# Attention block kernel: the stream of row maxima moved by 69 of a group's 144 events

## What is computed

```python
logits = jnp.einsum('bhqd,bhkd->bhqk', q, k) / jnp.sqrt(jnp.float32(HEAD))
causal = jnp.tril(jnp.ones((seq_len, seq_len), dtype=bool))
logits = jnp.where(causal[None, None], logits, -jnp.inf)
attn = jax.nn.softmax(logits, axis=-1)
o = jnp.einsum('bhqk,bhkd->bhqd', attn, v)
```

## Time and profile before

| what | value |
|---|---|
| median of 3 runs | 1465.85 us (1465.51 to 1467.76) |
| span of the profiled execution | 1465.0 us |
| mean granted TensorE clock of it | 0.921 |
| TensorE busy (matmuls) | 1309.6 us, 89% |
| VectorE busy | 1022.1 us, 70% |
| ScalarE busy | 773.8 us, 53% |
| prologue of the maxima | about 142 to 232 us |
| groups 0 to 7 | about 232 to 1112 us |

### The profile page before, as it was taken

How to read it: one execution, slowest core, us unless ns; L and a number is a source line. 1 busy time by engine, 2 the same in 40 slices (tenths; PEclk the granted TensorE clock), 3 DMA queues, 4 the chain that set the end, 5 groups by cost and what they waited for, 6 DMA issues and landing times. The chain is left out here.

```text
span 1465.0 us, 25799 instructions
## 1 busy us (share of the span) xinstructions
PE 1309.6 (89%) x8432; PEld 679.2 (46%) x8432; DVE 1022.1 (70%) x1862; ACT 773.8 (53%) x1009; POOL 172.6 (12%) x101
## 2 busy tenths in 40 slices
PE   4993899999999998999998999999994599999997
PEld 3872223333333333333433433433221588888886
DVE  4893997886886885886887688688300466666664
ACT  2771004665665664666565666566793244444443
POOL 1468100000000000000000000000001122222221
PEclk8996557999999999999999999999997699999999
DMA  6345400002102101200210300200003102222200
GB/s 204 123 165 165 131 1 11 21 16 58 33 18 50 40 17 35 56 19 15 65 26 4 74 18 16 63 6 5 10 8 91 44 1 58 58 57 57 57 14 29
DMA packets 75812, 71.07 MB, mean 49 GB/s; under 512 B 17816, under 2 KB 68704, under 8 KB 75688
## 3 DMA queue, kind: packets, MB, share of 16 engines
q1 hardware_dynamic: 75688, 69.51, 16.9%
HBM read 47.57 MB, written 21.23 MB: 47 GB/s over the span
## 5 line engine op out<-in xcount | busy, mean ns | idle before, releaser
L854 DVE TENSOR_REDUCE mx<-ps 128x1 f32<-128x512 f32 (+3 forms) x1120 | 692.2, 669 | 170.8 <-PE ps L726 105.8
L808 ACT ACTIVATE prob<-ps 128x1024 f32<-128x1024 f32 (+3 forms) x640 | 546.7, 895 | 413.8 <-PE ps L751 260.0
L723 PE MATMUL ps<-kst,qst 96*128 96x512 bf16 (+3 forms) x1280 | 426.4, 374 | 28.4 <-DMA kst<-qk_parts 24.3
L747 PE MATMUL ps<-qst,kst 99*128 99x512 bf16 (+3 forms) x1280 | 362.2, 355 | 11.2 <-issue 7.5
L763 PE MATMUL ps<-prob,vw 128*32 128x512 f32 (+3 forms) x2560 | 303.8, 547 | 0.2
L723 PEld LDWEIGHTS ps<-kst,qst 96*128 96x128 bf16 x1280 | 120.7, 99 | 334.7 <-DVE mx L854 244.9
L747 PEld LDWEIGHTS ps<-qst,kst 99*128 99x128 bf16 x1280 | 118.9, 99 | 147.5 <-ACT prob L808 51.1
L751 PE MATMUL ps<-mask_k,ident_bf 128*128 128x128 bf16 x512 | 106.2, 227 | 0.0
L726 PE MATMUL ps<-mask_q,ident_bf 128*128 128x128 bf16 x512 | 106.0, 232 | 0.0
L926 POOL COPY vw<-v_nat 128x1024 f32 (+1 forms) x8 | 8.3, 1044 | 766.3 <-PE ps L763 766.3
L763 PEld LDWEIGHTS ps<-prob,vw 128*32 128x32 f32 x2560 | 51.0, 109 | 102.0 <-issue 79.6
(11 more groups left out here) (144 smaller groups left out, 1429.5 us busy)
## 6 DMA issues: line engine op xcount, KB each, us to landing
qk_parts<-parts SPq DMA_DIRECT2D x32, 384.0 KB, 2.9
qst<-qk_parts SPq DMA_DIRECT2D x192, 64.0 KB, 2.6
kst<-qk_parts SPq DMA_DIRECT2D x192, 64.0 KB, 2.5
xs<-in_x SPq DMA_DIRECT2D x16, 512.0 KB, 6.3
o_rows<-o_sb SPq DMA_DIRECT2D x128, 32.0 KB, 1.7
o_raw<-o_rows SPq DMA_DIRECT2D x16, 256.0 KB
rd<-rden_rows SPq DMA_DIRECT2D x16, 256.0 KB
out<-y SPq DMA_DIRECT2D x8, 512.0 KB, 3.2
```

The source lines that it names most:

```text
L723: last = pe.matmul(at, q[0:QK_ROWS, J, h0 + h, i % 4 * P:(i % 4 + 1) * P], k[0:QK_ROWS, cb, h0 + h, 0:width], start=True, stop=not diagonal)
L747: last = pe.matmul(ps[:, h, 0:width], kst[c][0:ST_ROWS, t // 4, h, t % 4 * P:(t % 4 + 1) * P], qst[c][0:ST_ROWS, J, h, skip:BLK], start=Tr ...
L808: act.activation(prob[:, n % P_BUFS, 2 * pair:2 * pair + 2, 0:width], ps[:, 2 * pair:2 * pair + 2, 0:width], ACT.Exp).then_inc(exp_done, 1)
L854: dve.tensor_reduce(mx[:, h0:h0 + nh, i % 4, cb], ps[:, bank, 0:nh * width].rearrange("p (h x) -> p h x", h=nh), AX, ALU.max).then_inc(max ...
```

## The change

The stream of events is cut at event 69. The prologue holds events 0 to 68 of group 0. In group s the 120 slots hold events 69 to 143 of group s itself, then events 0 to 68 of group s + 1, spread evenly over all slots (1.2 per slot); group 7 holds only its own 75. So the turns of J = 2 and 3 (events 86 and 143) come in slots 14 and 62 of their own group, those of J = 0 and 1 (events 14 and 42) in slots 74 and 98 of the group ahead. `sync_step` has a new order to match, `invert` is called earlier in the stream of events, and the loads of group 1's queries and keys stand behind the maxima rows of J = 0 and 1 of group 0.

```diff
@@ -90,19 +74,21 @@
 EV = max_events()
 NEV = len(EV)
 assert NEV % S_BUFS == 0
-FIRST_SLOT = 7
 SLOTS_OF_TILE = 3
 
 
+
+AHEAD = 69
+TURN_EVENT = [EV.index(("turn", J)) for J in range(NJ)]
+NEAR_UNITS = [J for J in range(NJ) if TURN_EVENT[J] < AHEAD]
+OWN_UNITS = [J for J in range(NJ) if TURN_EVENT[J] >= AHEAD]
+INVERT_AT = NMU // 4
+
+
 def event_slots():
 
-    slots, done = [], 0
-    for u in range(SLOTS_OF_TILE * NKT):
-        want = min(NEV, max(0, (u - FIRST_SLOT) * NEV // (SLOTS_OF_TILE * NKT - FIRST_SLOT - 2)))
-        slots.append(range(done, want))
-        done = want
-    slots[-1] = range(slots[-1].start, NEV)
-    return slots
+    count = SLOTS_OF_TILE * NKT
+    return [range(u * NEV // count, (u + 1) * NEV // count) for u in range(count)]
 
 
 SLOTS = event_slots()
@@ -665,44 +651,59 @@
 
 
 
-            def sync_step(sp, s, c, hs, cur, nxt, far):
-                nhs = hs + c
-                nc_ = 1 - c
-                for J in range(NJ):
-                    if nxt:
-                        sp.wait_ge(max_red, (s + 1) * NEV + EV.index(("turn", J)) + 1)
-                        for a in range(NPART):
-                            sp.dma_start(qst[nc_][QK_ROWS + a:QK_ROWS + a + 1, J],
-                                         mT[a * 16:(a + 1) * 16, J, :]).then_inc(m_in[nc_][J], 16)
-                    if cur and far and J < NJ - 1:
-
+            def load_maxima(sp, s, c, J):
+
+                sp.wait_ge(max_red, s * NEV + TURN_EVENT[J] + 1)
+                for a in range(NPART):
+                    sp.dma_start(qst[c][QK_ROWS + a:QK_ROWS + a + 1, J],
+                                 mT[a * 16:(a + 1) * 16, J, :]).then_inc(m_in[c][J], 16)
+
+            def store_out(sp, s, c, hs, J):
+
+                sp.wait_ge(o_out, s * NJ + J + 1)
+                cols = slice(c * S + J * BLK, c * S + (J + 1) * BLK)
+                for h in range(GH):
+                    sp.dma_start(o_rows[bass.ds(hs * GH + h, 1), :, cols]
+                                 .rearrange("o r t -> (o r) t"),
+                                 o_sb[2 * HD * h:2 * HD * h + HD, J % 2, :]
+                                 ).then_inc(o_stored[J % 2], 16)
+
+                    sp.dma_start(den[32 * J + 8 * h:32 * J + 8 * h + 8, c, :],
+                                 o_sb[2 * HD * h + HD:2 * HD * h + HD + 1, J % 2, :]
+                                 ).then_inc(den_in[J % 2], 16)
+
+            def sync_step(sp, s, c, hs, nxt, far):
+
+                def queries(J):
+                    if far:
                         sp.wait_ge(st_done, s * 2 * NKT + 2 * (1 + max(n for n in range(NKT) if KT[n][0] == J)))
                         load_q(sp, c, hs + 1, J)
-                    if cur and far and J == NJ - 1:
-
-                        sp.wait_ge(st_done, (s + 1) * 2 * NKT)
-                        for j in range(NJ):
-                            load_k(sp, c, hs + 1, j)
-                        load_q(sp, c, hs + 1, J)
-                    if cur:
-                        sp.wait_ge(o_out, s * NJ + J + 1)
-                        cols = slice(c * S + J * BLK, c * S + (J + 1) * BLK)
-                        for h in range(GH):
-                            sp.dma_start(o_rows[bass.ds(hs * GH + h, 1), :, cols]
-                                         .rearrange("o r t -> (o r) t"),
-                                         o_sb[2 * HD * h:2 * HD * h + HD, J % 2, :]
-                                         ).then_inc(o_stored[J % 2], 16)
-
-                            sp.dma_start(den[32 * J + 8 * h:32 * J + 8 * h + 8, c, :],
-                                         o_sb[2 * HD * h + HD:2 * HD * h + HD + 1, J % 2, :]
-                                         ).then_inc(den_in[J % 2], 16)
-                    if cur and J == 1 and not (isinstance(s, int) and s == 0):
-                        store_rden(sp, s - 1, 1 - c, hs - 1 + c)
+
+                load_maxima(sp, s, c, OWN_UNITS[0])
+                for J in NEAR_UNITS:
+                    queries(J)
+                    store_out(sp, s, c, hs, J)
+                for J in OWN_UNITS[1:]:
+                    load_maxima(sp, s, c, J)
+                for J in OWN_UNITS[:-1]:
+                    queries(J)
+                    if nxt:
+                        load_maxima(sp, s + 1, 1 - c, NEAR_UNITS[0])
+                    store_out(sp, s, c, hs, J)
+                for J in NEAR_UNITS[1:]:
+                    if nxt:
+                        load_maxima(sp, s + 1, 1 - c, J)
+                if not (isinstance(s, int) and s == 0):
+                    store_rden(sp, s - 1, 1 - c, hs - 1 + c)
+                if far:
+                    sp.wait_ge(st_done, (s + 1) * 2 * NKT)
+                    for j in range(NJ):
+                        load_k(sp, c, hs + 1, j)
+                    load_q(sp, c, hs + 1, NJ - 1)
+                store_out(sp, s, c, hs, NJ - 1)
 
             def tensor_step(pe, s, c, hs, cur, nxt):
-                g, q, k = s + 1, qst[1 - c], kst[1 - c]
-
-                def event(e):
+                def event(g, gc, gh, e):
                     kind, w = EV[e]
                     bank = S_BANK + e % S_BUFS
 
@@ -716,12 +717,12 @@
                         return
                     J, i, h0, nh, cb, width, diagonal = MU[w]
                     if w == 0 or MU[w - 1][0] != J:
-                        pe.wait_ge(q_in[1 - c][J], loads(hs + c, Q_DMAS))
-                        pe.wait_ge(k_in[1 - c][J], loads(hs + c, K_DMAS))
+                        pe.wait_ge(q_in[gc][J], loads(gh, Q_DMAS))
+                        pe.wait_ge(k_in[gc][J], loads(gh, K_DMAS))
                     for h in range(nh):
                         at = ps[:, bank, h * width:(h + 1) * width]
-                        last = pe.matmul(at, q[0:QK_ROWS, J, h0 + h, i % 4 * P:(i % 4 + 1) * P],
-                                         k[0:QK_ROWS, cb, h0 + h, 0:width], start=True, stop=not diagonal)
+                        last = pe.matmul(at, qst[gc][0:QK_ROWS, J, h0 + h, i % 4 * P:(i % 4 + 1) * P],
+                                         kst[gc][0:QK_ROWS, cb, h0 + h, 0:width], start=True, stop=not diagonal)
                         if diagonal:
                             last = pe.matmul(at[:, width - P:width], ident_bf[:], mask_q[:],
                                              start=False, stop=True)
@@ -729,7 +730,10 @@
 
                 def maxima(slot):
                     for e in SLOTS[slot]:
-                        event(e)
+                        if AHEAD + e < NEV:
+                            event(s, c, hs, AHEAD + e)
+                        elif nxt:
+                            event(s + 1, 1 - c, hs + c, AHEAD + e - NEV)
 
                 def logits(n, pair):
                     J, t = KT[n]
@@ -766,22 +770,19 @@
                     last.then_inc(pv_done, 1)
 
                 if not cur:
-                    for e in range(NEV):
-                        event(e)
+                    for e in range(AHEAD):
+                        event(s + 1, 1 - c, hs + c, e)
                     return
                 for n in range(NKT):
                     logits(n, 0)
-                    if nxt:
-                        maxima(SLOTS_OF_TILE * n)
+                    maxima(SLOTS_OF_TILE * n)
                     if n >= PV_LAG:
                         values(n - PV_LAG, s, c)
                     elif not (isinstance(s, int) and s == 0):
                         values(NKT + n - PV_LAG, s - 1, 1 - c)
-                    if nxt:
-                        maxima(SLOTS_OF_TILE * n + 1)
+                    maxima(SLOTS_OF_TILE * n + 1)
                     logits(n, 1)
-                    if nxt:
-                        maxima(SLOTS_OF_TILE * n + 2)
+                    maxima(SLOTS_OF_TILE * n + 2)
                 if not nxt:
                     for n in range(NKT - PV_LAG, NKT):
                         values(n, s, c)
@@ -857,7 +858,7 @@
                         if w in LAST_MU:
                             dve.wait_ge(max_red, g * NEV + e + 1)
                             make_parts(LAST_MU[w])
-                        if w == NMU // 2 and not (isinstance(s, int) and s <= 0):
+                        if w == INVERT_AT and not (isinstance(s, int) and s <= 0):
                             invert(dve, s - 1, 1 - c)
                     assert count[0] == per_s
 
@@ -878,17 +879,18 @@
                 for J in range(NJ):
                     load_q(sp, 0, 0, J)
                     load_k(sp, 0, 0, J)
+                for J in NEAR_UNITS:
+                    load_maxima(sp, 0, 0, J)
                 for J in range(NJ):
                     load_q(sp, 1, 0, J)
                     load_k(sp, 1, 0, J)
-                sync_step(sp, -1, 1, -1, False, True, False)
-                sync_step(sp, 0, 0, 0, True, True, True)
+                sync_step(sp, 0, 0, 0, True, True)
                 with sp.Fori(0, (NG - 4) // 2) as k:
```

(10 more changed lines are left out.)

## The result

The changed kernel takes 1416.2 us (median of 3 runs, 1415.77 to 1416.47) against 1465.85: a ratio of 0.9653, 95% interval 0.9636 to 0.9671. That is 49.6 us less, where 29.4 were forecast. The profiled execution spans 1414.0 us.

The account below looks back on a forecast made before the run. TensorE was taken as the bound in middle groups, VectorE in the late prologue. Terms -45.9 + 16.2 - 6.5 - 3.2 + 2 + 3 + 5 = -29.4 gave 1436.4 us against the median; range 1423 to 1454.

Parts of the forecast that it names:

- step 8: Full tiles: spreading events evenly, 3.6 a tile instead of 4, costed at nothing.
- step 4: Turn of J 3, seven groups: logits before it cut the pause from 1.96 to about 1.5 us, -3.2 us.
- step 7: Middle of groups: pauses among full tiles lower the clock in three of ten cases, +5 us (bounds 0 and 17).
- Step 1: Prologue: only 69 events remain, so group 0 starts near 186.2 instead of 232.1, -45.9 us.
- Step 2: Group 7: 75 events in tiles 0 to 20 make it 96.0 us against 79.8, +16.2 us.
- Step 3: Starts of groups: low clock in groups 1, 2, 6 and group 4's wait for keys go, -6.5 us.
- step 6: Middle of groups 3 and 5: VectorE's loop ends make TensorE idle 1.5 us each, +3 us.
- Step 5: Start of group 0: low clock as before (7.9 us), now with events in these tiles, +2 us.
- Step 9: SyncE's queue: maxima loads arrive in time for tile 12, with 2 to 5 us of cover.
- Rival B: Turns of J 0 to 2: spread dissolves their waits (8.4 us), no clock falls (-5): 1423 us, chance 0.12.
- Rival A: Full tiles: all ten pauses bring the low clock, VectorE's loop ends cost in full: 1452 us, chance 0.16.
- Rival C: Group 0: clock doesn't rise, all of it runs at 1.2 GHz: 1531 us, chance 0.04.

Follow-up runs that it names:

- run 3: Changed kernel with its shift by 69 events but the old uneven slots (first eight empty, then 1.3 events a slot): 1434.35 us.
- run 4: Changed kernel with the old uneven slots, and the turn of J 3 one slot later, behind a pair of logits: 1433.74 us.
- run 1: Changed kernel with the turn of J 3 moved into the slot of its last unit, no logits between: 1424.99 us.
- run 6: Changed kernel with VectorE's three passes written out, no loop; other engines keep theirs: 1412.95 us.
- run 7: Changed kernel with the passes of TensorE, ScalarE and VectorE written out, no loops there: 1402.42 us.
- run 2: Kernel before the change, with the turn of J 3 behind the first logits of the next group: 1462.83 us.
- run 10: Kernel with all three engines' loops written out, turns of J 0 to 2 four units behind their last unit instead of three: 1399.79 us.
- 9 (with loops): Changed kernel, loops kept, with 67 events ahead instead of 69: 1415.89 us.

## Why the prediction was wrong in its size

**The step that failed is 8**: "The even spread ... is costed at nothing: TensorE is the bound and its work is the same." The work is the same, but TensorE, which works through its queue in order, also stands still wherever it meets a wait, and how the events are spread decides on how long (in runs 3 and 4 the attention stage, with the same matmuls, ends 17.8 and 21.0 us later than in the changed kernel). Without the even spread the forecast would have held: the shift alone gives 32.4 us in run 3 and 32.7 in run 4, where 29.4 were forecast, and run 4, whose pause of 1.6 us is nearest to step 4's 1.5, has four falls of the clock behind turns, where step 7 took three. The even spread is worth some 18 us more. It has no term of its own in the measured times; it appears inside the others, which for groups 0 to 6 were forecast to add 0.3 us and in fact took 19.7 away:

- Step 1, the prologue: -45.9 forecast, -46.3 measured.
- Step 2, group 7: +16.2 forecast, +14.1 measured (80.7 to 94.8 us up to the end of its last values). The 19 tiles without events took 38.3 us in both kernels; the first 21 took 56.6 and not 58.7.
- Step 3, the starts of groups: -6.5 forecast. Low clock and other idle time together went from 12.8 to 4.5 us in groups 1 to 6, and 1.5 of these 4.5 are step 6; so about -9.8. The stops at TensorE's loop ends became 0.9 shorter besides.
- Step 4, the turns' waits: -3.2 forecast for seven groups, -7.5 measured in groups 1 to 6 alone (the table's first row). The pause of J 3 shrank as worked out, 1.96 to 1.4, 3.3 of the 7.5. Missed were the waits of the other turns (-1.4) and of the matmuls right behind the turns (-2.8).
- Step 5, group 0's start: +2 forecast. The clock rose after 3.3 us (189.1), not 7.9; by the same working as in the table its low stretch cost 1.6 instead of 3.4 us (half of each length bounds it, 1.7 and 4.0), so the term is about -1.8. The wrong assumption was that the time at the low clock stays the same when events fill these tiles.
- Step 6, VectorE's loop ends: +3 forecast, about +1.5 measured (1.2 of it idle time for banks). VectorE idled 2.86 us there.
- Step 7, pauses among full tiles: +5 forecast, nothing measured, 0 falls behind 8 turns. Run 1 shows that the danger is real: with 0.55 us more of pause six of eight are followed by it. The term came to nothing with a pause of 1.4; at 1.6, in run 4, the clock fell behind four of eight turns.

Step 9 held: in the changed kernel no tile waited for maxima, and with 60 events ahead tile 24 does. Rival B would have given 1423. Of its two parts the one came true, no fall of the clock; of the other, 8.4 us by transposes of J 0 to 2 that no longer wait, one transpose in three stopped waiting, and their waits fell by 1.4 us in groups 1 to 6. Rivals A, C and D did not occur. The range was cut at rival B, as if its parts were all that could be missed on that side; a bound for step 8 was not set at all, though the earlier trace rows show VectorE near enough to TensorE in a full tile for order to matter. The rule of the Trainium skill ("Runtime: NRT & Kernel Launch", Instruction fetch mechanics) on taken branches agrees with runs 6 and 7: the stops go when the loops are written out. VectorE did pay its own stop (2.86 us), as by that rule, but TensorE only 0.5 to 0.6 of it for banks. The one on the clock ("TensorE: Matmul & The Clock Gate", What's actually happening) agrees with group 0: with the denser stream the clock rose after 3.3 us, with the first slots empty it took 6.4 us or more. The prologue does not fit so simply: from 186.2 to 232.1 in the kernel before it was 0.50 throughout, with TensorE busy 42.3 of 45.9 us.

## What to carry to other kernels

An engine that is the bound and works in order still has waits in it; before an even spread of a second engine's work is costed at nothing, count the bound engine's excess over its usual intervals, since that is what order can win. A spread and a shift may only work together: the one needs data that the other brings in time, so try them apart before crediting either. Where short pauses are followed by a lower clock, put other work of the same engine between the two ends of the dependence, and look at what waits next (keys in run 2, banks in run 10).

## What was not expected of the hardware

TensorE's clock falls behind pauses in a way that the length alone doesn't settle. Over the turns of J 3 in the runs with shifted events: behind pauses of 0.9 to 1.4 us it never fell (48 turns in six kernels), behind pauses of 1.6 to 2.05 us in 23 of 40 turns, in the same program in some groups and not in others (1.6 us: 4 of 8; 1.8 us: 5 of 8; 1.96 us: 6 of 8 and 2 of 8; 2.05 us: 6 of 8). A fall took the clock to 0.50 for 3.4 us, in the kernel with 60 events ahead mostly for 6.8 (five of six), and one of 3.4 cost 0.6 to 1.6 us in run 1. Behind the stops of 2.9 to 3.4 us at loop ends the low stretch was 3.4 us twice in the changed kernel, 6.8 twice with only VectorE's loop written out, and one of each in runs 3, 4 and 9 (with loops). What decides between the two was not tried.

The best kernel that ran is that with the three loops written out and 67 events ahead: 1398.57 us, 17.6 below the changed kernel and 67.8 below the kernel before it, measured beside it (1466.4). The one with four units of lag, 1399.79, can't be told from it.
